# Attention: the Newton steps of the norms' inverse roots move from VectorE to GpSimd, and Q and K are projected three batches ahead

## The reference, cut to what matters

```python
def proj(W, b):
    return (x @ W.T + b).reshape(B, T, H, dk).transpose(0, 2, 1, 3)
Q = proj(Wq, bq)
K = proj(Wk, bk)
V = proj(Wv, bv)
Qn = Q / jnp.maximum(jnp.linalg.norm(Q, axis=-1, keepdims=True), EPS)
Kn = K / jnp.maximum(jnp.linalg.norm(K, axis=-1, keepdims=True), EPS)
scores = jnp.einsum('bhqd,bhkd->bhqk', Qn, Kn) / jnp.sqrt(jnp.float32(dk))
attn = jax.nn.softmax(scores, axis=-1)
head_outs = jnp.einsum('bhqk,bhkd->bhqd', attn, V)
...
head_outs = head_outs * (gate_static * gate_dynamic)
out = head_outs.transpose(0, 2, 1, 3).reshape(B, T, D)
return out @ Wo.T + bo
```

## Time and profile before

| | us |
|---|---|
| median of 3 runs | 1359.31 |
| lowest and highest | 1352.22, 1359.81 |
| the profiled execution: its time | 1357.14 |
| the profiled execution: its span | 1355.3 |
| attention, from VectorE's first clearing of `vext` to its last addition | 134.9 to 534.2 |
| one body of attention in the middle (L780 to L780) | 11.83 |

### The profile page before, as it was taken

How to read it: one execution, slowest core, us unless ns; L and a number is a source line. 1 busy time by engine, 2 the same in 40 slices (tenths; PEclk the granted TensorE clock), 3 DMA queues, 4 the chain that set the end, 5 groups by cost and what they waited for, 6 DMA issues and landing times. The chain is left out here.

```text
span 1355.3 us, 26991 instructions
## 1 busy us (share of the span) xinstructions
PE 1158.9 (86%) x9434; PEld 830.1 (61%) x9434; DVE 951.6 (70%) x3021; ACT 675.0 (50%) x1087; POOL 584.3 (43%) x524
## 2 busy tenths in 40 slices
PE   0781699999999997999999997999599898978884
PEld 0560355555555553899999894777456676666663
DVE  7917899999999994567666662888674488843231
ACT  1761377777777774444444342555333266533330
POOL 2300133333333332455555552333348478427776
PEclk9885699999999998999999998999789999989997
DMA  9350400000000001122222222222349112344443
GB/s 314 131 176 4 175 26 24 26 24 24 26 24 26 24 26 33 54 71 70 70 71 71 65 67 64 75 63 67 100 142 291 39 57 67 116 135 64 63 64 30
DMA packets 89567, 103.50 MB, mean 76 GB/s; under 512 B 12860, under 2 KB 75004, under 8 KB 89340
## 3 DMA queue, kind: packets, MB, share of 16 engines
q1 hardware_dynamic: 68768, 74.61, 17.4%
q0 software_dynamic: 19968, 26.63, 8.4%
q10 hardware_dynamic: 732, 0.94, 0.2%
HBM read 55.52 MB, written 46.63 MB: 75 GB/s over the span
## 5 line engine op out<-in xcount | busy, mean ns | idle before, releaser
L1029 POOL DMA_INDIRECT slots<-rowbuf,slots x192 | 193.8, 1009 | 346.8 <-ACT probs L841 327.3
L841 ACT ACTIVATE probs<-ps 128x1024 f32<-128x1024 f32 x256 | 255.2, 1025 | 96.0 <-PE ps L751 96.0
L1139 POOL DMA_INDIRECT y<-slot_y,where x144 | 150.1, 1042 | 144.6 <-DVE slot_y L1120 121.0
L1200 ACT ACTIVATE slot_h<-ps,own 128x256 f32<-128x256 f32 x288 | 120.5, 470 | 151.7 <-PE ps L1171 150.0
L1171 PE MATMUL ps<-slot_x,own 128*128 128x256 f32 x576 | 140.4, 388 | 3.0 <-DVE slot_x L1109 3.0
L1183 PEld LDWEIGHTS ps<-own,slot_h 128*128 128x128 f32 x1152 | 139.8, 192 | 3.6
L1183 PE MATMUL ps<-own,slot_h 128*128 128x128 f32 x1152 | 140.1, 275 | 0.0
L767 PE MATMUL ps<-probs,vext 128*32 128x256 f32 x2048 | 137.8, 387 | 0.0
L1614 POOL DMA_INDIRECT out<-xT,where x64 | 99.3, 1551 | 40.3 <-DVE xT L1917 25.1
L1171 PEld LDWEIGHTS ps<-slot_x,own 128*128 128x128 f32 x576 | 105.4, 193 | 18.1 <-DVE slot_x L1109 6.5
L1765 ACT ACTIVATE h<-ps,packs 128x512 f32<-128x512 f32 x64 | 44.0, 687 | 91.7 <-PE ps L1666 89.9
(11 more groups left out here) (301 smaller groups left out, 2237.2 us busy)
## 6 DMA issues: line engine op xcount, KB each, us to landing
toeplitz<-conv_kernel SPq DMA_DIRECT2D x16, 1024.0 KB, 7.3
slots<-blank SPq DMA_DIRECT2D x26, 528.0 KB, 7.2
slot_rows<-slots SPq DMA_DIRECT2D x72, 132.0 KB, 2.2
routed<-y SPq DMA_DIRECT2D x32, 256.0 KB, 3.2
packs<-in_experts SPq DMA_DIRECT2D x1, 4624.0 KB, 14.2
packs<-in_experts SPq DMA_DIRECT2D x8, 578.0 KB, 7.6
xT<-slots SPq DMA_DIRECT2D x16, 264.0 KB, 2.6
out<-stream SPq DMA_DIRECT2D x16, 256.0 KB, 2.3
```

Of the source, the lines that this page charges most:

```text
L841: act.activation(probs[:, p % 4, :, :, :].rearrange("p j k t -> p j (k t)"), ps[:, 2 * (p % 2):2 * (p % 2) + 2, :], ACT.Exp, scale=DK ** - ...
L1029: return pool.indirect_dma_start(m["slot_dram"][layer], bass.IndirectOffsetOnAxis(ap=where, axis=0), m["rowbuf"][:, tile, :], None)
L1139: pool.indirect_dma_start(m["y_dram"][layer], bass.IndirectOffsetOnAxis(ap=where[:, j, h:h + 1], axis=0), y[:, j, h, :], None).then_inc(se ...
L1200: ins = act.activation(hidden[:, j % 2, k, :], ps[:, 2 * (j % 2) + k // 2, (k % 2) * LOT:(k % 2) * LOT + LOT], act_func, bias=own[:, j, P_ ...
```

## The change

The three Newton steps leave VectorE. `inverse_roots` becomes `first_guess` (the same four instructions), called by `seed`, and GpSimd runs `newton`: per step four instructions, since the fused one is split in two, each waiting for the one before. `qk`, `rn` and `root` get two buffers. Every part that prepares Q and K up to the guess runs one batch further ahead (b + 3), while `unit` and `cut_high` stay at b + 2 and now wait for `rooted`. GpSimd calls `newton(b + 3)` between its second and third scatter of batch b. The bodies start at -3.

```diff
-        qk = sb("qk", [P, 2, 2 * D])
+        qk = sb("qk", [P, 2, 2, 2 * D])
         sq = sb("sq", [P, 2, 2 * D])
-        rn, guess, root = sb("rn", [P, 4 * H]), sb("guess", [P, 4 * H]), sb("root", [P, 4 * H])
+        rn, root = sb("rn", [P, 2, 4 * H]), sb("root", [P, 2, 4 * H])
+        guess, factor = sb("guess", [P, 4 * H]), sb("factor", [P, 4 * H])
...
-            for b in range(-2, B + 1):
+            for b in range(-3, B + 1):
                 body(b)
...
             def project_qk(b):
-                if has(b - 2):
-                    pe.wait_ge(sem["v_taken"], b - 1)
+                if has(b - 3):
+                    pe.wait_ge(sem["v_taken"], b - 2)
...
-                pe.wait_ge(sem["qk_ready"], min(b + 2, B))
+                pe.wait_ge(sem["qk_ready"], min(b + 3, B))
...
-                if has(b + 2):
-                    project_qk(b + 2)
+                if has(b + 3):
+                    project_qk(b + 3)
...
         def _(pool):
+            def newton(b):
+                pool.wait_ge(sem["seeded"], b + 1)
+                c = Chain(pool, sem["newton"], b * 4 * NEWTON)
+                x, y = rn[:, b % 2, :], root[:, b % 2, :]
+                for _ in range(NEWTON):
+                    c.link(pool.tensor_tensor(factor[:, :], y, y, ALU.mult))
+                    c.link(pool.tensor_tensor(factor[:, :], factor[:, :], x, ALU.mult))
+                    c.link(pool.tensor_scalar(factor[:, :], factor[:, :], 1.5, None, ALU.add))
+                    c.link(pool.tensor_tensor(y, y, factor[:, :], ALU.mult))
+                pool.engine_nop().then_inc(sem["rooted"], 1)
...
-            pool.wait_ge(m["cleared"], 16 * SPARE)
-            pool.wait_ge(m["blanked"], 16 * len(BLANK_CHUNKS))
-            for b in range(B):
-                for n in range(4):
-                    scatter(b, n)
+            for b in range(-3, B):
+                if b == 0:
+                    pool.wait_ge(m["cleared"], 16 * SPARE)
+                    pool.wait_ge(m["blanked"], 16 * len(BLANK_CHUNKS))
+                if has(b):
+                    scatter(b, 0)
+                    scatter(b, 1)
+                if has(b + 3):
+                    newton(b + 3)
+                if has(b):
+                    scatter(b, 2)
+                    scatter(b, 3)
...
-            def roots(b):
+            def seed(b):
                 dve.wait_ge(sem["summed"], b + 1)
-                inverse_roots(Chain(dve, sem["norms"], b * ROOT_STEPS), rn, guess, root)
+                first_guess(Chain(dve, sem["seeds"], b * SEED_STEPS), rn[:, b % 2, :], guess[:, :], root[:, b % 2, :])
+                dve.engine_nop().then_inc(sem["seeded"], 1)
 
             def unit(b):
+                dve.wait_ge(sem["rooted"], b + 1)
...
-                if has(b + 2):
-                    take_qk(b + 2)
+                if has(b + 3):
+                    take_qk(b + 3)
...
-                if has(b + 2):
-                    squares(b + 2)
+                if has(b + 3):
+                    squares(b + 3)
...
-                if has(b + 2):
-                    roots(b + 2)
+                if has(b + 3):
+                    seed(b + 3)
```

More of the change, by code:

```diff
@@ L63 @@
 NEWTON = 3
-ROOT_STEPS = 4 + 3 * NEWTON
+SEED_STEPS = 4
 EPS = 1e-5
@@ L682, in attention @@
             ("loaded", "v_zero", "v_ready", "qk_projected", "qk_ready", "v_projected", "v_taken", "squared", "summed",
-                "norms", "normal", "highs", "stacked", "q_turned", "k_turned", "q_taken", "k_taken", "scores",
+                "seeds", "seeded", "newton", "rooted", "normal", "highs", "stacked", "q_turned", "k_turned", "q_taken", "k_taken", "scores",
                 "probs", "pv", "oT_ready", "out_turned", "rsum", "on_ready", "on_turned", "onT_ready", "mixed", "added",
@@ L887, in take_qk @@
                 wide = rows[:, R_BQKV:R_BQKV + 2 * D].unsqueeze(1).broadcast_to([P, 2, 2 * D])
-                dve.tensor_tensor(qk[:, :, :], ps[:, IN, :].rearrange("p (t n) -> p t n", t=2), wide, ALU.add)\
+                dve.tensor_tensor(qk[:, b % 2, :, :], ps[:, IN, :].rearrange("p (t n) -> p t n", t=2), wide, ALU.add)\
                    .then_inc(sem["qk_ready"], 1)
@@ L902, in squares @@
                 dve.wait_ge(sem["qk_ready"], b + 1)
-                dve.tensor_tensor(sq[:, :, :], qk[:, :, :], qk[:, :, :], ALU.mult).then_inc(sem["squared"], 1)
+                dve.tensor_tensor(sq[:, :, :], qk[:, b % 2, :, :], qk[:, b % 2, :, :], ALU.mult).then_inc(sem["squared"], 1)
                 dve.wait_ge(sem["squared"], b + 1)
-                dve.tensor_reduce(rn[:, :], sq[:, :, :].rearrange("p t (h d) -> p (t h) d", d=DK),
+                dve.tensor_reduce(rn[:, b % 2, :], sq[:, :, :].rearrange("p t (h d) -> p (t h) d", d=DK),
                                   AX.X, ALU.add).then_inc(sem["summed"], 1)
-            def roots(b):
+            def seed(b):
                 dve.wait_ge(sem["summed"], b + 1)
-                inverse_roots(Chain(dve, sem["norms"], b * ROOT_STEPS), rn, guess, root)
+                first_guess(Chain(dve, sem["seeds"], b * SEED_STEPS), rn[:, b % 2, :], guess[:, :], root[:, b % 2, :])
+                dve.engine_nop().then_inc(sem["seeded"], 1)
             def unit(b):
+                dve.wait_ge(sem["rooted"], b + 1)
                 dve.tensor_tensor(sq[:, :, :].rearrange("p t (h d) -> p (t h) d", d=DK),
-                                  qk[:, :, :].rearrange("p t (h d) -> p (t h) d", d=DK),
-                                  root[:, :].unsqueeze(2).broadcast_to([P, 4 * H, DK]),
+                                  qk[:, b % 2, :, :].rearrange("p t (h d) -> p (t h) d", d=DK),
+                                  root[:, b % 2, :].unsqueeze(2).broadcast_to([P, 4 * H, DK]),
                                   ALU.mult).then_inc(sem["normal"], 1)
@@ L1439, in moments, with first_guess @@
     dve.tensor_scalar(rstd, mv[:, :, 1], eps, None, ALU.add).then_inc(sem["raised"], 1)
-def inverse_roots(c, x, guess, root):
+def first_guess(c, x, guess, root):
     dve, bits = c.engine, mybir.dt.int32
[L1447 to L1455, removed]
+    c.link(dve.tensor_scalar(x, x, TINY, None, ALU.max))
+    c.link(dve.tensor_scalar(guess.bitcast(bits), x.bitcast(bits), 1, None, ALU.logical_shift_right))
+    c.did(dve.tensor_scalar(root.bitcast(bits), guess.bitcast(bits), -1.0, float(0x5f3759df), ALU.mult, ALU.add))
+    c.link(dve.tensor_scalar(x, x, -0.5, None, ALU.mult))
 def inverse_root(pool, sem, g, rstd, power):
```

## The result

The changed kernel takes 1341.76 us in the median of 4 runs (1340.66 to 1343.67), the kernel before 1358.12 beside it (4 runs). The ratio is 0.9887, with a 95% interval of 0.9862 to 0.9912: 1.1% faster. The forecast was 1361 us, no change. The time lies at the lower edge of the range and where the first rival (VectorE not held) put it, at 1342.

A forecast was written before the change was run, and what follows sets the result against it. VectorE was taken as the bound, TensorE 0.70 us behind. A body of 11.22 + 0.65 = 11.87 us against 11.83 gave 29 x 0.04 + 2.0 - 1.2 = +2.0 us; forecast 1361 us, range 1341 to 1392.

The forecast's parts named there:

- the first rival: In attention, VectorE is not held by GpSimd: a body takes 11.22 us, the kernel 1342 us; chance 0.17.
- The bound and the cap: In attention, VectorE bounds and TensorE stands 0.70 us behind, so a body gains 0.7 us or less.
- `rooted` is no wait: In attention, `unit` comes a body after the seed, leaving `newton` 15 us for its 4.2, so no wait.
- The start: Start of attention: batch 0's Newton steps take 4.2 us on GpSimd against 2.33 on VectorE; +2.0 us, bounds 0 and +5.
- Body 29: Near the end of attention: without `project_qk` it should go as body 30 did, in 10.62 us: -1.21.
- GpSimd's price: Twelve linked instructions at 0.35 us make 4.2 per body; with scatters 5.1 and 0.5 handing over, 9.8 us.
- The second rival: GpSimd is the bound in attention: kernel 1378 us at d = 0.57, about 1458 at d = 0.79; chance 0.10.
- d = 0.52: Cost in us of one linked GpSimd instruction at which GpSimd's body time passes 11.83 us.
- 5 x 0.13 = 0.65 us per body: GpSimd holds `unit` and the four casts on VectorE 0.13 us each, in the loop; ends 0 and 1.4.
- the wrong case: L1887 in the earlier trace: GpSimd got in between VectorE's successive instructions; cited against VectorE not being held.
- The third rival: Port in full: `unit` and four casts each held 0.28 us, 1.4 per body; body 12.62, kernel 1383 us; chance 0.25.
- Its worst case: VectorE let in at none of GpSimd's links, `unit` waits about 2 us: 13.2 us per body, 1400 us.

The follow-up runs named there:

- the fourteen products without links: Changed kernel with fourteen GpSimd products of 128x64, none waiting for another, in place of the twelve linked Newton instructions: 1354.77 us, ratio 0.9984 to the kernel before.
- the same fourteen products: Changed kernel with fourteen GpSimd products of 128x64, each waiting for the one before, in place of the Newton steps: 1351.05 us, ratio 0.9966 to the kernel before.
- one step fewer: Changed kernel with the first of three Newton steps back on VectorE, two left on GpSimd: 1342.06 us, beside 1339.79 for the unaltered changed kernel.
- four of 128x512: Changed kernel with four linked GpSimd products of 128x512 over constants in place of the Newton steps: 1394.03 us, ratio 1.0302 to the kernel before.

## Why the prediction was wrong

**The bound and the cap were right.** TensorE 0.70 us behind VectorE, a loop of 11.22 without holds: the floor measured is 11.12 with either distance, the changed kernel stands at 11.19. The loop was 0.10 too long because its 2.71 us from `take_v` to `turn_out` held a delay by a scatter that is gone in the changed kernel (2.61 without Newton steps). That shedding 2.34 us from VectorE buys at most 0.7 is shown by the kernel before without Newton steps.

**`rooted` is no wait** in the middle: right, `unit` comes 7.2 us after `newton` ends. Without the third batch it is the bound, 13.83 us.

**The start was right at +2.0 us, in part by luck.** `newton` of batch 0 takes 144.29 - 139.02 = 5.3 us, not 4.2. Set beside the starts without Newton steps, the third batch costs 30.5 - 27.3 = 3.2 us, GpSimd's steps 32.7 - 30.5 = 2.2, and 3.4 are saved on VectorE: +2.0 in sum, but not the +1.9 of batch 0's roots with batch 1 for nothing.

**Body 29 did not go as body 30:** it took 11.30 us, so that the term is -0.5, not -1.2. It has lost `project_qk`, but VectorE still has `unit` and the casts of batch 31 to do, which body 30 of the kernel before had not; TensorE waits 1.00 us for `oT` there. Without Newton steps it takes 11.11 us, so 0.19 are GpSimd's holds.

**GpSimd's price was low.** A linked instruction costs 0.40 us, not 0.35; with its waits for VectorE, `newton` takes 5.98 us, not 4.2. GpSimd needs 11.1 us, not 9.8. I see no effect of this on the time, but the room I saw was not there: a fourth step makes GpSimd the bound. The second rival was nearer than its 0.10 said; its d = 0.52 stands against 0.50 measured with conflicts.

**The step that failed** is "5 x 0.13 = 0.65 us per body". The size of a hold was right: 0.11 to 0.13 in the fourteen products without links. The count was wrong. I let each of five VectorE instructions meet a GpSimd instruction under way. In the changed kernel only two GpSimd instructions fall on the five, and both find VectorE on the port first: they wait 0.54 and 0.22 us, VectorE 0.07 in all. Of the 0.68 us by which a body is shorter than the forecast's 11.87, the holds are 0.58 and the loop's length 0.10. The sum with the measured body is 29 x (-0.64) + 2.0 - 0.5 for body 29 = -17.1, 1342 us. (The two traces give some 16 us; there body 0 is part of the start.)

Why the count is small: with a link, GpSimd's next instruction comes only 0.08 us after the end of the one before, and by then VectorE's next has the port. Two readings bear on this. Without links the loop pays 0.49. With links between the same fourteen products it pays 0.13 to 0.28, in part because fewer of them fall on `unit` and the casts. That is shown for the first bodies of one experiment only; that it holds at any phase is not, since in its later bodies scatters hold the casts and one step fewer made the loop longer. The changed kernel's low cost is thus also a matter of where its steps fall: in its early body from 175.04 on, `unit` and a cast are held and the stretch is 2.86 us. From the earlier trace rows I had taken the wrong case: L1887 was held by instructions of about 1 and 1.26 us, and the two that ran back to back had no link. The third rival's time for a body comes out with long instructions, 12.67 us with four of 128x512, but by two holds of some 0.8 us and not by its five of 0.28. Its worst case, `unit` waiting for a whole run of GpSimd's, is the one late body without links.

## What to carry to other kernels

Ask first how far the next engine is behind: here 2.34 us taken from the bound were worth 0.7 at most. For work moved to an engine that shares a port, don't multiply the hold by the instructions it might meet: count how many of the other engine's instructions fall on the loop that sets the pace, and see who is there first. Short instructions that wait for one another left the port to VectorE here; long ones, or ones without waits between, took it from the loop. And move the consumer a round away when the receiving engine is slower, then check that this engine's total stays under the period. Where an experiment makes a kernel slower, look at the granted clock of each body before you put all of the time down to the wait.

## What the hardware showed that I had not expected

A scatter on GpSimd, not only its arithmetic, can hold a float32 to float16 cast: one cast took 683 ns instead of 280 when a scatter had started before it. (The Trainium skill describes the other direction in the same section of "SBUF — State Buffer": while VectorE copies in a mode that uses the shared port, GpSimd cannot write the descriptors of its DMAs. Scatters do take longer beside VectorE here, 1.43 us instead of 0.96 with four Newton steps, where one starts at 310.78 beside `unit` and the casts; which of them delays it no run shows.) In the kernel before, the same meeting cost up to 0.22 (504 against 288 ns), and it was already in its body: the last cast's 0.12 us of delay was part of the 2.71 us. GpSimd's lag may feed back on this. In the changed kernel the second scatter of a batch ran 4.8 us behind its exponential, at the same distance in 25 successive bodies, with no idle time on GpSimd but the gaps between instructions. I take it that the waits for VectorE shrink or grow with the phase until GpSimd's round fits the body; no experiment tests that.

Nor had I expected TensorE's clock to move in the experiments. In the middle of the stage it stayed at 1.00 where TensorE waited up to 0.9 us a body for `oT` (four Newton steps), and fell in two kernels where it waited longer: 2.6 us without the third batch (13.83 us a body, 15.3 to 16.4 in eleven), 1.5 us with the products of 128x512 (12.67 us, 14.2 in six).
